# A macaron block in step order: start-up loads cut into other pieces, and the first norm's transposes put at the end of the step before

## The reference

```python
x = x + 0.5 * ffn(layernorm(x), We, be, Wg, bg)      # 8 experts of 256x256, the top 2 by gate
x = x + attn(layernorm(x), Wp, bp, Wq, bq, Wk, bk, Wv, bv, Wo, bo)
x = x + 0.5 * ffn(layernorm(x), We, be, Wg, bg)      # the same weights again
```

## Time and profile before

| what | value |
|---|---|
| median of 3 runs | 1085.39 us (1084.07 to 1086.07) |
| the profiled execution's own time | 1085.55 us |
| its span | 1083.7 us |
| PE busy | 1007.0 us, 93% |
| DVE busy | 868.4 us, 80% |
| POOL busy | 634.2 us, 59% |
| ACT busy | 464.8 us, 43% |
| DMA | 23.51 MB, mean 22 GB/s |

### The profile page before, as it was taken

The page is one execution under the profiler, slowest core; times in us unless marked ns, Lnnn a source line. Parts: engine busy times, 40 slices in busy tenths (PEclk is TensorE's granted clock), DMA queues, the critical chain, the costliest instruction groups (busy, mean ns, idle before and its releaser), DMA issues.

```text
span 1083.7 us, 16805 instructions
## 1 busy us (share of the span) xinstructions
PE 1007.0 (93%) x5102; PEld 827.0 (76%) x5102; DVE 868.4 (80%) x2324; ACT 464.8 (43%) x1052; POOL 634.2 (59%) x891
## 2 busy tenths in 40 slices
PE   1189999999999999999999999999999999999875
PEld 1067877888888888888888888888888888888664
DVE  1245888898888888988888888988888889888783
ACT  1035453454444444444444444444444444444332
POOL 2036656766666667666666667666666676554443
PEclk9999999999999999999999999999999999999998
DMA  3201100000000000000000000000000000000000
GB/s 88 93 19 30 36 14 21 20 20 16 7 20 21 21 20 20 20 21 3 19 21 20 20 21 20 21 16 6 21 20 21 20 20 20 11 11 1 11 19 21
DMA packets 13954, 23.51 MB, mean 22 GB/s; under 512 B 2715, under 2 KB 7315, under 8 KB 13863
## 3 DMA queue, kind: packets, MB, share of 16 engines
q1 hardware_dynamic: 10358, 14.42, 3.8%
q0 software_dynamic: 3088, 8.00, 2.5%
q10 hardware_dynamic: 418, 0.01, 0.0%
HBM read 12.99 MB, written 8.39 MB: 20 GB/s over the span
## 4 chain that ended last, share of the span: by engine, by line
PE 83%; DVE 7%; SPq 5%; issue 2%; POOL 1%; DMA 1%; ACT 0%; POOLq 0%; ACTq 0%; DVEq 0%
PE ffn_bank L952 20%; PE ffn_bank L954 19%; PE ffn_bank L953 19%; PE tr_bank L989 5%; PE mix_bank L952 4%; PE mix_bank L954 4%; PE mix_bank L953 4%; SPq L231 3%; PE tr_bank L1004 3%; PE tr_bank L952 1%; PE tr_bank L953 1%; PE tr_bank L954 1%; SPq L238 1%; DVE chain_sum L696 1%; PE tr_bank L1011 1%
## 5 line engine op out<-in xcount | busy, mean ns | idle before, releaser
L952 PE MATMUL ffn_bank<-we_hi,T_hi 128*128 128x512 f32 x1024 | 410.3, 401 | 13.4 <-DVE we_lo L796 7.2
L954 PE MATMUL ffn_bank<-we_hi,T_lo 128*128 128x512 f32 x1024 | 401.3, 392 | 0.0
L953 PE MATMUL ffn_bank<-we_lo,T_hi 128*128 128x512 f32 x1024 | 400.9, 392 | 0.0
L460 ACT ACTIVATE we_raw<-ffn_bank,gate 128x256 f32<-128x256 f32 x512 | 210.1, 469 | 186.0 <-PE ffn_bank L954 171.8
L327 POOL TENSOR_TENSOR chain_sum<-chain_sum,we_raw 128x512 f32<-128x512 f32 x128 | 165.9, 1296 | 199.2 <-DVE chain_sum L696 198.8
L952 PEld LDWEIGHTS ffn_bank<-we_hi,T_hi 128*128 128x128 f32 x1024 | 193.4, 189 | 57.9 <-DVE chain_sum L696 12.0
L954 PEld LDWEIGHTS ffn_bank<-we_hi,T_lo 128*128 128x128 f32 x1024 | 193.2, 189 | 42.2
L953 PEld LDWEIGHTS ffn_bank<-we_lo,T_hi 128*128 128x128 f32 x1024 | 193.7, 189 | 35.4
L696 DVE SCALAR_TENSOR_TENSOR chain_sum<-ffn_bank,gate,we_raw 128x256 f32<-128x256 f32 x256 | 111.2, 474 | 48.4 <-ACT we_raw L460 40.0
L315 POOL TENSOR_TENSOR var_eps<-mean_var,eps 128x2 f32<-128x2 f32 x96 | 27.8, 290 | 197.9 <-DVE mean_var L624 197.9
L696 DVE SCALAR_TENSOR_TENSOR chain_sum<-ffn_bank,gate,chain_sum 128x256 f32<-128x256 f32 x256 | 111.1, 475 | 19.7 <-PE ffn_bank L954 17.9
(11 more groups left out here) (111 smaller groups left out, 1468.1 us busy)
## 6 DMA issues: line engine op xcount, KB each, us to landing
out_x<-y SPq DMA_DIRECT2D x31, 256.0 KB
we_last<-in_L_ffn_We SPq DMA_DIRECT2D x4, 256.0 KB
we_raw<-in_L_ffn_We SPq DMA_DIRECT2D x4, 256.0 KB
we_raw<-in_L_ffn_We SPq DMA_DIRECT2D x4, 254.0 KB
x_in<-in_L_attn_x,x_row POOLq DMA_INDIRECT x60
x_in<-in_L_attn_x SPq DMA_DIRECT2D x2, 256.0 KB, 4.6
moved_qk<-qk SPq DMA_DIRECT2D x4, 124.0 KB
w_raw<-in_L_attn_Wp SPq DMA_DIRECT2D x1, 256.0 KB, 16.8
```

Source lines behind the costliest of these rows:

```text
L460: last = nc.scalar.activation(scaled[:, f, t, half, j], ffn_bank[b][:, j * D:(j + 1) * D], ACT.Copy, scale=gate[:, 2 * f + t, e:e + 1])
L952: nc.tensor.matmul(dest, hi[:, t, k, :], w_hi_[:, k, c0:c1], start=(first and k == 0), stop=False, skip_group_check=not first)
L953: nc.tensor.matmul(dest, hi[:, t, k, :], w_lo_[:, k, c0:c1], start=False, stop=False, skip_group_check=not first)
L954: last = nc.tensor.matmul(dest, lo[:, t, k, :], w_hi_[:, k, c0:c1], start=False, stop=(k == KB - 1), skip_group_check=not first)
```

## The change

The loads of We's second block are cut otherwise: 112 rows per bank, and the last 15 rows of all eight experts by one transfer that goes out before the banks. Wg comes in one transfer of 128 partitions, and its bias through a tile of its own (`wg_bias`, zeroed by GpSimd) that VectorE adds; VectorE's subtraction of the last row becomes one instruction. From pair 6 on, the first norm's transposes stand at the end of step n-2, behind TD and TB, and write `mix_bank[1]`; `hi_step` and `lo_step` keep their places in ScalarE's and VectorE's order and read from there, and the second q, k product of a step waits until that bank has been read.

```diff
@@ -126,7 +126,7 @@
         w_raw = sb("w_raw", [PART, 5, KB, D])
         we_last = sb("we_last", [PART, E * D])
         wT, wp = sb("wT", [PART, KB, 3 * D]), sb("wp", [PART, KB, D])
-        wg_raw = sb("wg_raw", [PART, KB, E])
+        wg_raw, wg_bias = sb("wg_raw", [PART, KB, E]), sb("wg_bias", [PART, E])
 
         x_in = sb("x_in", [PART, 4, 2, D])
         stats = sb("stats", [PART, 3, 2, 6])
@@ -169,6 +169,14 @@
         flat_bank, logit_bank = tr_bank[1][0:NF * 2 * E, 0:2 * PART], tr_bank[1][:, 2 * PART:4 * PART]
         proj_bank, v_bank = tr_bank[1], mix_bank[0]
 
+        def ta_late(n):
+
+            return n.const >= 6
+
+        def bank_of(i, n):
+            return mix_bank[1] if i == TA and ta_late(n) else t_bank[i]
+
+
 
         w_loaded, wp_loaded = sem("w_loaded"), sem("wp_loaded")
         bp_loaded, bqkv_loaded = sem("bp_loaded"), sem("bqkv_loaded")
@@ -225,15 +233,19 @@
         @block.sync
         def _(sp):
             sp.dma_start(x_in[:, 0, :, :], x_tiles[:, 0:2, :]).then_inc(x_loaded[0], 16)
+
+            most_rows = 7 * (PART // 8)
             sp.dma_start(we_raw[PART - 1:PART, 1, :], be.rearrange("(o e) n -> o (e n)", o=1)).then_inc(be_loaded, 16)
+            sp.dma_start(we_raw[most_rows:PART - 1, 1, :].rearrange("p (e n) -> p e n", e=E),
+                         We[:, PART + most_rows:LAST, :].rearrange("e p n -> p e n")).then_inc(be_loaded, 16)
             for b in range(4):
                 at, experts = slice(b * BANK, (b + 1) * BANK), slice(2 * b, 2 * b + 2)
                 sp.dma_start(we_last[:, at].rearrange("p (e n) -> p e n", e=2),
                              We[experts, LAST, :].partition_broadcast(PART)).then_inc(we_loaded[b], 16)
                 sp.dma_start(we_raw[:, 0, at].rearrange("p (e n) -> p e n", e=2),
                              We[experts, 0:PART, :].rearrange("e p n -> p e n")).then_inc(we_loaded[b], 16)
-                sp.dma_start(we_raw[0:PART - 1, 1, at].rearrange("p (e n) -> p e n", e=2),
-                             We[experts, PART:LAST, :].rearrange("e p n -> p e n")).then_inc(we_loaded[b], 16)
+                sp.dma_start(we_raw[0:most_rows, 1, at].rearrange("p (e n) -> p e n", e=2),
+                             We[experts, PART:PART + most_rows, :].rearrange("e p n -> p e n")).then_inc(we_loaded[b], 16)
             for w, W in ((4, Wp), (0, Wq), (1, Wk), (2, Wv), (3, Wo)):
                 sp.dma_start(w_raw[:, w, :, :], W.rearrange("(k p) n -> p k n", p=PART)).then_inc(
                     w_loaded if w < 4 else wp_loaded, 16)
@@ -285,6 +297,7 @@
 
         @block.gpsimd
         def _(pool):
+            nc.gpsimd.memset(wg_bias[:], 0.0)
             nc.gpsimd.memset(ident[:], 0.0).then_inc(ident_set, 1)
             pool.wait_ge(ident_set, 1)
             nc.gpsimd.affine_select(out=ident[:], in_=ident[:], compare_op=ALU.not_equal, fill=1.0, base=0,
@@ -409,10 +422,10 @@
         @block.scalar
         def _(act):
 
-            act.dma_start(wg_raw[:, 0, :], Wg[0:PART, :]).then_inc(wg_loaded, 16)
-            act.dma_start(wg_raw[0:PART - 1, 1, :], Wg[PART:LAST, :]).then_inc(wg_loaded, 16)
-            act.dma_start(wg_raw[PART - 1:PART, 1, :], bg.rearrange("(o e) -> o e", o=1)).then_inc(wg_loaded, 16)
+            act.dma_start(wg_raw[:], Wg.rearrange("(k p) e -> p k e", p=PART)).then_inc(wg_loaded, 16)
             act.dma_start(wg_last[:], Wg[LAST, :].partition_broadcast(PART)).then_inc(wg_loaded, 16)
+            act.wait_ge(ident_set, 1)
+            act.dma_start(wg_bias[PART - 1:PART, :], bg.rearrange("(o e) -> o e", o=1)).then_inc(wg_loaded, 16)
 
             def hi_step(i, n):
                 act.wait_ge(T_done[i], n.times(1, 1))
@@ -423,7 +436,7 @@
                     await_(act, v_done, n.times(1))
                 else:
                     await_(act, proj_done, n.times(1))
-                nc.scalar.copy(halves(i, n)[0][:].rearrange("p t k n -> p (t k n)"), t_bank[i][:, :]).then_inc(hi_done[i], 1)
+                nc.scalar.copy(halves(i, n)[0][:].rearrange("p t k n -> p (t k n)"), bank_of(i, n)[:, :]).then_inc(hi_done[i], 1)
 
             def flat_step(g):
                 act.wait_ge(flat_done, g.times(1, 1))
@@ -496,7 +509,7 @@
                 nc.scalar.copy(we_hi[:, :, b * BANK:(b + 1) * BANK], we_raw[:, :, b * BANK:(b + 1) * BANK]).then_inc(we_hi_done, 1)
 
             def first_body(s):
-                act.wait_ge(wg_set, 1)
+                act.wait_ge(wg_set, 2)
                 act.wait_ge(consts_set, 1)
                 for f in range(NF):
                     last = nc.scalar.copy(wg[:, f, :, f, 0].bitcast(f32r), wg_raw[:])
@@ -626,7 +639,7 @@
             def lo_step(i, n):
                 dve.wait_ge(hi_done[i], n.times(1, 1))
                 hi, lo = halves(i, n)
-                nc.vector.tensor_tensor(lo[:].rearrange("p t k n -> p (t k n)"), t_bank[i][:, :],
+                nc.vector.tensor_tensor(lo[:].rearrange("p t k n -> p (t k n)"), bank_of(i, n)[:, :],
                                         hi[:].rearrange("p t k n -> p (t k n)").bitcast(f32),
                                         ALU.subtract).then_inc(lo_done[i], 1)
 
@@ -798,11 +811,12 @@
             def first_body(s):
                 dve.wait_ge(consts_set, 1)
                 stats_step(LN1, s + 1)
-                dve.wait_ge(wg_loaded, 16 * 4)
-                nc.vector.tensor_tensor(wg_raw[:, 0, :], wg_raw[:, 0, :], wg_last[:], ALU.subtract)
-                nc.vector.tensor_tensor(wg_raw[0:PART - 1, 1, :], wg_raw[0:PART - 1, 1, :], wg_last[0:PART - 1, :],
+                dve.wait_ge(wg_loaded, 16 * 3)
+                nc.vector.tensor_tensor(wg_raw[:], wg_raw[:], wg_last[:].unsqueeze(1).to_broadcast([PART, KB, E]),
                                         ALU.subtract).then_inc(wg_set, 1)
-                dve.wait_ge(be_loaded, 16)
+                dve.wait_ge(wg_set, 1)
+                nc.vector.tensor_tensor(wg_raw[:, 1, :], wg_raw[:, 1, :], wg_bias[:], ALU.add).then_inc(wg_set, 1)
+                dve.wait_ge(be_loaded, 32)
                 we_set_step(0)
                 dve.wait_ge(wg_hi_done, 1)
                 for f in range(NF):
@@ -969,7 +983,9 @@
                     await_(pe, lo_done[TB], after_pair(s - 1))
                 else:
                     pe.wait_ge(normed_done[{TA: LN1, TB: LN2, TD: LN3}[i]], n.times(2, 2))
-                    if i == TA and s.const == 0:
+                    if i == TA and ta_late(n):
+                        pe.wait_ge(qk_copied, (n - 2).times(2))
+                    elif i == TA and s.const == 0:
                         pe.wait_ge(wqkv_lo_done, KB)
                     if i == TA:
                         await_(pe, gate_ops, s.times(GATE_OPS, 2) if s.const >= 0 else 0)
@@ -986,7 +1002,7 @@
                 for t in range(2):
                     for k in range(KB):
                         at = (t * KB + k) * PART
-                        last = nc.tensor.transpose(t_bank[i][:, at:at + PART], source[:, t, k * PART:(k + 1) * PART], ident[:])
+                        last = nc.tensor.transpose(bank_of(i, n)[:, at:at + PART], source[:, t, k * PART:(k + 1) * PART], ident[:])
                 last.then_inc(T_done[i], 1)
 
             def logits_step(s):
@@ -1038,6 +1054,8 @@
                     await_(pe, v_copied, n.times(1))
                 else:
                     await_(pe, qk_copied, n.times(2))
+                    if ta_late(n + 2):
+                        await_(pe, lo_done[TA], min(n.const + 3, PAIRS))
                 product(mix_bank[t][:, :], TB, n, t, wqkv_hi, wqkv_lo, 0, 2 * D).then_inc(qk_done, 1)
 
             def v_step(n):
@@ -1125,8 +1143,6 @@
                     pe.wait_ge(lo_done[TD], 1)
                 elif s.within(PAIRS):
                     ffn_step(FFN1, s, s, 0)
-                    if (s + 1).within(PAIRS):
-                        T_step(TA, s + 1, s)
                     ffn_step(FFN1, s, s, 1)
                 logits_step(s)
                 if drained:
@@ -1165,6 +1181,8 @@
                     ffn_step(FFN2, s - 4, s, 1, range(2 if drained else 1, 4))
                 if s.within(PAIRS):
                     T_step(TB, s, s)
+                if (s + 2).within(PAIRS):
+                    T_step(TA, s + 2, s)
 
             def fill_body(s):
                 if s.const >= 0:
```

## The result

The changed kernel takes 1045.83 us (median of 4 runs, 1043.76 to 1046.50) against 1084.73 us (4 runs) for the kernel before: a ratio of 0.9638, 95% interval 0.9619 to 0.9657, 38.9 us less. The forecast was 1047. Its profiled execution has a span of 1044.6 us, 39.1 less than 1083.7.

The account below looks back on a forecast made before the run. TensorE, busy 93% of the span, bounds the kernel, except at the start, where it waits for Wo behind one-engine loads. From 1085.55: - 37.1 (Wo) - 1.0 (clock) + 0 (transposes) = 1047.5, said as 1047 us; 8-in-10 range 1043 to 1054.

Parts of the forecast that it names:

- What bound the start: Start: each 127-partition load runs on one DMA engine and blocks SyncE's issues; TensorE waits 21.1 us for Wo.
- The loads after: Start: 18 units of 256 KB at 0.95 us each land Wo at 20.1 us, gaining 37.1 us (34.4 to 40).
- What is late next: Start: VectorE's bank chain, from bank 0 at 7.2 us to 22.8, costs nothing, with 2.7 us of room.
- The cap: Start: VectorE keeps bank 3 from starting before 22.8 us, so the gain is not more than 39.8 us.
- the rival with the quick start: Start: early upper clock and quick loads, VectorE's chain then limits the gain; 1043 to 1045.6 us, chance 0.15.
- The clock: Start: TensorE may reach its upper clock earlier, gaining nothing to 2.3 us; 1.0 taken.
- The moved transposes: Steps of pairs 6 to 31: moving them costs 0, bounds -0.05 to +0.1 us a step, -1.3 to +2.6 us in all.
- The waits that weren't new: Steady steps: TensorE, busy 560.00 of 560.00 us, is not made to wait; the steady part costs nothing.
- the new wait of the second q, k product: Each step: the product waits for `lo_done[TA]`, with 6.6 us of room.
- the transposes' input: Step's end: the first norm of pair s+2 is written at 474.78 and needed at 478.4, 3.6 us of room.
- The narrowest room: FFN2, bank 1: `chain_step` ends 0.2 us before TensorE writes the bank; both ends move together, so it stays.
- The start's gain carried whole to the end: After the start: nothing waits for the loads after Wo, so the whole start gain reaches the end.

Follow-up runs that it names:

- two_engines: Changed kernel with the banks' second blocks cut at 122 rows in place of 112 (5 rows in the transfer ahead): 1062.00 us, ratio 0.9803 to the kernel before.
- no_broadcast: Changed kernel with we_last filled from 128 different rows of We, not one row broadcast to all partitions (wrong expert weights): 1044.3 us, one run.
- loads_only: Changed kernel with its loads kept and the first norm's transposes put back between the FFN halves: 1047.52 us, ratio 0.9663 to the kernel before.
- mid_mix: Changed kernel with the transposes back between the FFN halves but still written to the second Q,K bank: 1047.30 us, ratio 0.9657 to the kernel before.
- chain_mid: Changed kernel with VectorE's FFN2 chain_step on bank 1 ahead of score_step, except in the drain: 1043.45 us, ratio 0.9607 to the kernel before.

## Why the prediction was right, point by point

**What bound the start** was right. The 127-row load ran on one engine and held SyncE; with 112 rows no issue is long, and two_engines shows that the divisor sets it. What the new Wg loads or the transfer of 15 rows do by themselves wasn't run.

**The loads after**: Wo's transposes start at 21.35, not at 20.1; the gain at Wo's wait is 57.17 - 21.35 = 35.8 us where 37.1 were worked out. The term that was off is the rate of 0.95 us a unit from 2.3 us on. From 2 to 6 us the streams moved 185 GB/s and not 275, in the second half of it, by no_broadcast, because of the broadcast row. The rate had been read from 50 to 54 us, where matrices and x pass and no row is broadcast to all partitions. The 0.7 us for the completion was an estimate without a row.

**What is late next** was right in kind: VectorE's chain. Its first bank came at 9.47 in place of 7.2, its pace was 3.54 us a bank where the earlier trace rows gave 3.63, so its end was 24.81 and not 22.8. The forecast gave it 2.7 us of room and said that it costs nothing; it had none, and bank 3 waits 0.16 us for it. The cap was thus not 39.8 but 62.58 - 24.86 = 37.7 us, and it is what the start gave. This is the mechanism of the rival with the quick start, the VectorE cap, though the loads weren't quick. The sum ran over Wo, and the path that set the start ran over bank 0. An earlier Wo alone would have won nothing (no_broadcast).

**The clock** gave more than the 1.0 us taken. Wo to bank 3 takes 3.5 us in place of 5.4, and would have taken 24.54 - 21.35 = 3.2 without the wait for VectorE: 2.2 us, nearly the upper bound of 2.3, of which VectorE took 0.3 back. The sum of the two, 35.8 + 1.9 = 37.7, stood in the forecast as 38.1. That it came so near is luck: 1.3 us too much for Wo and 0.9 too little for the clock nearly cancel.

**The moved transposes** were taken as 0, bounds -0.05 to +0.1 us a step. They gave (30.64 + 30.78 - 30.60 - 30.70) / 2 = 0.06 us a step, 1.6 us over 26, just outside the bound. The error is in the reading of the earlier trace rows: 0.45 for four and 0.90 for eight transposes looked like no price per block, but the rows were read only as far as the second matmul behind them. About half of what is won, 0.03 us a step, stands in starts that are given to two decimals, spread over the block and the matmuls behind it. The other half is the wait for ScalarE on bank 0, 0 to 0.06 us a step, which the forecast has nowhere; of step 14's 0.90, 0.02 are this wait. loads_only and mid_mix show that the gain goes with the place, not with the bank or the start. With it the whole gain in the traces is 39.1 us where the sum had 38.1.

**The waits that weren't new** were right in the main: the windows have TensorE busy 560.00 of 560.00 us still, and neither the new wait of the second q, k product nor the transposes' input appears in the list of waits. The narrowest room, in FFN2, was judged at 0.2 us from step 14, the other kind of step; in every second step it is less than nothing, before as after, and chain_mid turns that into 2.2 us. A busy share of 100% hides such waits, since a matmul's busy time overlaps the next one's.

**The start's gain carried whole to the end**: the difference is 39.32 at step 31 and 39.28 at step 35.

## What to carry to other kernels

A load whose partition count isn't a multiple of 16 is cut into a part that is and a small rest; 127 rows cost some 37 us here and 122 still 16, and the cut costs one small transfer more. When a long wait goes, work out the chain that is second and take its rates from the same stretch and the same kind of transfer. A reordering that pays in the steady steps is tried without the drain as well: the same edit lost there all that it had won, and kept 2.2 us without it. And before two traces are compared, see that they don't differ in a stretch that varies from one execution to the next, as the clock does here behind a wait.

## What the runs showed of the hardware

- A DMA's engines by its row count: 127 rows showed a DMA share of 0.07 at 24 GB/s, 122 rows 0.13 at 48 GB/s and long issues of 4 to 5.4 us in place of 8.8 to 10.7, 112 rows no issue above 1.4 us.
- Loading one row into all partitions lowers the rate of the whole mixture: 182 GB/s at a share of 0.86 with it (182 to 222 in ten traces), 329 at 1.02 without (one), in the same 2 us.
- With little but transposes and gate products before 15.04 us, TensorE ran FFN bank 0 at the lower clock, and it came to the upper one within bank 1 (distance 0.23 from 18.7); 1.5 us of waiting for Wo didn't send it back. In two_engines, with 2 us of waiting between the two banks, both ran at the lower clock to their end.
- After a wait of 2.1 to 2.5 us between the marks of steps 4 and 5, TensorE ran some matmuls at the lower clock in ten of thirteen traces, which cost 1.3 to 1.6 us, and stayed at the upper one in three.
- Joining two blocks of transposes saves some 0.03 us, whatever bank they write (12.25 to 12.22 us).
